# Layer-norm scale of a conditioned FFN: root and reciprocal replaced by a power and a diagonal sum on GpSimd

## The chip, the cores and the metric

The kernel runs on one core of one Trainium2 chip. The metric is the time of one execution on the device in microseconds (us).

## The reference

Input x has 4 sequences of 1024 rows with D = 1024 columns. All arithmetic is float32.

```python
xr = x.reshape(Bx, Tx, 8, LATENT)                                # LATENT = 128
h = jnp.einsum('btel,elf->btef', xr, W1) + b1                    # 8 experts, 128 -> 512
h = jax.nn.gelu(h, approximate=False)
y = (jnp.einsum('btef,efl->btel', h, W2) + b2).reshape(Bx, Tx, Dx)   # 512 -> 128
eo = jax.nn.silu(emb) @ emb_W + emb_b
scale, shift = jnp.split(eo[:, None, :], 2, axis=-1)
# _layernorm: (h - mu) * jax.lax.rsqrt(var + 1e-5) * g + b, over the 1024 columns
hn = _layernorm(y, ln_g, ln_b) * (1.0 + scale) + shift
return x + jax.nn.silu(hn) @ out_W + out_b
```

## The kernel before

Every matmul is made from three float32r products: each operand is split into a high and a low part (names ending in `_hi` and `_lo`), ScalarE or VectorE rounds the high part and VectorE subtracts it for the low part. The order of every engine's work is written out by hand in its own block, with counting semaphores between them.

**First stage (to about 354 us).** 32 items n, one for each of the 8 groups g and 4 sequences t; each has 4 steps c over the 512 hidden columns, so 128 steps m. For a step TensorE runs `first` (W1, L923) and `second` (W2, L939), ScalarE the gelu (L489), VectorE the split of its result (L663, L665). A finished item, a transposed block of y with 128 columns by 1024 rows, goes to `y_scratch` in DRAM. Between the steps VectorE computes dot products for the conditioning vector.

**Second stage (from about 354 us).** y is transposed here: columns lie on the partitions. A pair p is 256 rows of y (two row tiles q = 2p and 2p + 1), a tile of 128 partitions x 8 groups x 256. There are 16 pairs and 32 row tiles. For a pair:

- VectorE sums the 8 groups into `mean_total` (L738 to L748), GpSimd sums that over the partitions (L427, `mean_of`), so every partition has the sum for each of the 256 rows; VectorE subtracts the mean (`centre`, L753).
- ScalarE squares (L509), VectorE sums into `var_total` (L758 to L766), GpSimd sums over the partitions into `var_all` (L434, `var_of`).
- ScalarE takes the root of var / D + eps (`root`, L523), for which it changes its table before and after (L519, L601, and L559 for pair 0); VectorE takes the reciprocal (`invert`, L770) and multiplies both halves of y by it (`norm`, L775).
- ScalarE applies scale, shift and silu (L589) and rounds (L514), VectorE makes the low part (`rest_s`, L793).
- TensorE multiplies with out_W (`project`, L949), 48 matmuls for a row tile q; the last row tile is cut into pieces (`project_pieces`, L1001). VectorE adds the result to x (`finish`, L868), x having been given the bias by a DMA with addition from GpSimd's queue (`add_bias`, L440).

VectorE's loop over i is what sets the order. Pass i does: `finish(2i - 1)`, the inverse and norm of pair i + 1, the mean sums of pair i + 2, the low part of the first half of pair i + 1, `finish(2i)`, the centring of pair i + 2, the low part of the second half, the variance sums of pair i + 2. `finish` also holds the tail sums (L698): products for the conditioning vectors of the last two sequences, three ahead of an odd q and one ahead of an even q up to q = 12, then one or two up to q = 19. TensorE starts row tile q when `finish(q - 2)` is done and, for even q, when the low part of its pair is there. GpSimd's loop does in pass i `mean_of(i + 2)`, `add_bias(2i + 2)`, `var_of(i + 2)`, `add_bias(2i + 3)`. Pairs 0 and 1 are done beside the first stage, at items written out one by one (the norm of pair 0 at item 27, before the splits of later steps).

## Time and profile before

| what | value |
| --- | --- |
| median of 3 runs | 706.13 us (706.08 to 706.57) |
| span of the profiled execution, first to last instruction | 704.2 us |
| TensorE busy | 700.5 us, 99% of the span |
| VectorE busy | 603.7 us, 86% |
| ScalarE busy | 469.3 us, 67% |
| GpSimd busy | 104.1 us, 15% |
| moved by DMA | 133.22 MB, 189 GB/s on average |
| chain that ended last | TensorE 99% of the span |

The profile is of one execution. Its span leaves out what lies around the first and the last instruction; the median of the runs is the time with that. The names of lines are those of the program before. An engine's busy share says how full it is over the whole span; which wait counts is read from the timelines of one pass and from the chain. In a timeline, what stands in square brackets is the time for which the engine was idle before the row and what ended it.

### The profile page before, as it was taken

What the parts mean: (1) busy time and instruction counts of PE and PEld (TensorE: products, weight loads), DVE (VectorE), ACT (ScalarE), POOL (GpSimd) and SP (SyncE); (2) the same over time, 40 slices, a digit from 0 to 9 for tenths busy, and PEclk for the clock granted to TensorE, in tenths of its full rate; (3) what the DMA queues carried; (4) which work ended last, traced back from release to release, by engine and by line L of the source; (5) the groups of instructions that cost most, each with busy time, mean ns of one, the idle gap of its engine ahead of it and who ended that gap; (6) DMA issues with size and microseconds to landing.
All of it is one profiled execution on the core that took longest, in us unless ns stands there. A gap on an engine that the chain in (4) does not pass through costs nothing.

```text
span 704.2 us, 8302 instructions
## 1 busy us (share of the span) xinstructions
PE 700.5 (99%) x3082; PEld 577.9 (82%) x3082; DVE 603.7 (86%) x725; ACT 469.3 (67%) x526; POOL 104.1 (15%) x68
## 2 busy tenths in 40 slices
PE   9999999999999999999999999999999999999998
PEld 6888888888888888888888888888888888888887
DVE  6888999999999989899887999999999978677512
ACT  7898888888878879888883456454656454555500
POOL 0000000000000011100121332423232432322100
PEclk9999999999999999999999999999999999999999
DMA  6766557344232531332789687887699877565531
GB/s 240 247 232 207 187 203 231 109 169 150 90 121 90 209 120 61 120 107 104 210 293 301 183 279 233 275 256 246 219 293 264 256 217 210 183 176 143 156 120 60
DMA packets 51880, 133.22 MB, mean 189 GB/s; under 512 B 4096, under 2 KB 25216, under 8 KB 49408
## 3 DMA queue, kind: packets, MB, share of 16 engines
q1 hardware_dynamic: 46944, 115.79, 46.9%
q0 software_dynamic: 4608, 16.78, 12.3%
q8 instruction: 24, 0.39, 0.2%
q10 hardware_dynamic: 288, 0.13, 0.1%
q14 instruction: 16, 0.13, 0.1%
HBM read 82.35 MB, written 33.55 MB: 165 GB/s over the span
## 4 chain that ended last, share of the span: by engine, by line
PE 99%; DMA 0%; ACT 0%; DVE 0%; issue 0%; DVEq 0%
PE psum L949 48%; PE psum L939 25%; PE psum L923 25%; PE psum L1001 2%; DMA wraw<-in_W 0%; PE psum L971 0%; ACT W L534 0%; DVE res L901 0%; DVEq L125 0%
## 5 line engine op out<-in xcount | busy, mean ns | idle before, releaser
L665 DVE TENSOR_TENSOR g_lo<-g_raw,g_hi 128x1024 fp32r<-128x1024 f32 x128 | 158.4, 1239 | 27.9 <-ACT g_hi L495 25.3
L489 ACT ACTIVATE g_raw<-psum,cols 128x1024 f32<-128x1024 f32 x128 | 142.9, 1116 | 34.1 <-PE psum L923 24.9
L949 PE MATMUL psum<-oW_hi,s_lo 128*128 128x512 f32 x496 | 152.7, 389 | 0.0
L949 PE MATMUL psum<-oW_hi,s_hi 128*128 128x512 f32 x496 | 152.7, 389 | 0.0
L949 PE MATMUL psum<-oW_lo,s_hi 128*128 128x512 f32 x496 | 152.6, 389 | 0.0
L939 PE MATMUL psum<-g_hi,W 128*128 128x512 f32 x512 | 136.8, 389 | 0.0
L923 PE MATMUL psum<-xT_hi,W 128*128 128x512 f32 x508 | 135.8, 389 | 0.0
L939 PEld LDWEIGHTS psum<-g_hi,W 128*128 128x128 f32 x512 | 96.1, 188 | 20.0
L923 PEld LDWEIGHTS psum<-xT_hi,W 128*128 128x128 f32 x508 | 95.3, 188 | 19.8
L949 PEld LDWEIGHTS psum<-oW_hi,s_hi 128*128 128x128 f32 x496 | 93.1, 188 | 19.4
L949 PEld LDWEIGHTS psum<-oW_hi,s_lo 128*128 128x128 f32 x496 | 93.1, 188 | 19.3
L949 PEld LDWEIGHTS psum<-oW_lo,s_hi 128*128 128x128 f32 x496 | 93.1, 188 | 19.3
L589 ACT ACTIVATE yb<-yb,mod_c,mod_a 128x256 f32<-128x256 f32 x120 | 62.3, 590 | 56.6 <-DVE yb L775 56.6
L427 POOL PARTITION_ALL_REDUCE mean_all<-mean_total x16 | 41.2, 2576 | 384.0 <-DVE mean_total L748 384.0
L939 PE MATMUL psum<-g_lo,W 128*128 128x512 f32 x256 | 78.8, 389 | 0.0
L868 DVE TENSOR_TENSOR res<-psum,res 128x1024 f32<-128x1024 f32 x31 | 37.8, 1219 | 47.6 <-PE psum L949 47.6
L923 PE MATMUL psum<-xT_lo,W 128*128 128x512 f32 x254 | 78.2, 389 | 0.0
L495 ACT CAST g_hi<-g_raw 128x1024 fp32r<-128x1024 f32 x63 | 66.3, 1052 | 8.1 <-PE psum L939 6.7
L509 ACT ACTIVATE sq<-yb 128x1024 f32<-128x1024 f32 x32 | 34.0, 1062 | 36.6 <-DVE yb L753 35.6
L434 POOL PARTITION_ALL_REDUCE var_all<-var_total x16 | 35.8, 2237 | 144.0 <-DVE var_total L766 144.0
L698 DVE SCALAR_TENSOR_TENSOR tail_out<-tail_cols,tail_cond 128x1024 f32<-128x1024 f32 x32 | 52.4, 1666 | 4.6 <-DMA tail_cols<-in_emb_T 4.6
L939 PEld LDWEIGHTS psum<-g_lo,W 128*128 128x128 f32 x256 | 47.9, 188 | 10.1 <-DVE g_lo L665 0.2
(77 smaller groups left out, 679.8 us busy)
## 6 DMA issues: line engine op xcount, KB each, us to landing
y_scratch<-y_stage SPq DMA_DIRECT2D x32, 512.0 KB, 3.1
yb<-y_scratch SPq DMA_DIRECT2D x16, 1024.0 KB, 4.8
res<-in_x SPq DMA_DIRECT2D x32, 512.0 KB, 6.1
res<-out_b_all POOLq DMA_DIRECT2D x32, 512.0 KB, 4.5
xT_raw<-in_xT SPq DMA_DIRECT2D x31, 512.0 KB, 4.3
out<-res SPq DMA_DIRECT2D x31, 512.0 KB, 4.1
tail_cols<-in_emb_T SPq DMA_DIRECT2D x24, 512.0 KB, 7.2
wraw<-in_out_W SPq DMA_DIRECT2D x16, 256.0 KB, 4.9
```

Source lines behind the costliest of these rows:

```text
L427: nc.gpsimd.partition_all_reduce(mean_all[:], mean_total[:], P, bass.bass_isa.ReduceOp.add).then_inc(mean_done, 1)
L434: nc.gpsimd.partition_all_reduce(var_all[:], var_total[:], P, bass.bass_isa.ReduceOp.add).then_inc(var_done, 1)
L489: nc.scalar.activation(g_raw[:, m % 2], ring(m), ACT.Gelu, bias=cols[:, R_B1 + k:R_B1 + k + 1]).then_inc(gelu_done, 1)
L495: nc.scalar.copy(g_hi[:, m % 2], g_raw[:, m % 2]).then_inc(ghi_act, 1)
L509: nc.scalar.activation(sq[:, half_of(h)], yb[p % 3][:, half_of(h)], ACT.Square).then_inc(squared, 1)
L589: nc.scalar.activation(yb[p % 3][:, g], yb[p % 3][:, g], ACT.Silu, scale=mod_a[:, b, g:g + 1], bias=mod_c[:, b, g:g + 1]).then_inc(silu_do ...
L665: nc.vector.tensor_tensor(g_lo[:, m % 2], g_raw[:, m % 2], g_hi[:, m % 2].bitcast(F32), ALU.subtract).then_inc(glo_done, 1)
L698: nc.vector.scalar_tensor_tensor(tail_out[i % 2][:], tail_cols[l % SLOTS][:], 1.0, tail_cond[:, b - EARLY], ALU.mult, ALU.mult, accum_out= ...
L868: nc.vector.tensor_tensor(res[:, q % 4], proj(q), res[:, q % 4], ALU.add).then_inc(out_ready, 1)
L923: mm = nc.tensor.matmul(ring(m)[:, half], W[:, g % WS, w, cut], v[:, n % 2, half], start=(k == 0), stop=(k == 2))
L939: mm = nc.tensor.matmul(y_psum(n)[:, half], W[:, g % WS, w, cut], v[:, m % 2, half], start=(c == 0 and k == 0), stop=(c == C - 1 and k == 2))
L949: mm = nc.tensor.matmul(proj(q)[:, half], v[:, g, cut], w[:, g, half], start=(g == 0 and k == 0), stop=(g == G - 1 and k == 2))
```

## The change

`root` on ScalarE and `invert` on VectorE go. GpSimd, after its sum over the partitions, issues a DMA that takes the 256 values of one partition and lays them out as two per partition (`var_spread`, 128 x 2), scales them and adds eps, takes them to the power -0.5, writes them onto a diagonal (`rstd_diag`, 128 x 256, zero but for the two columns that belong to the partition), and sums that over the partitions, so that every partition again has all 256 values (`rstd`). `norm` reads `rstd` from SBUF for every pair. The outputs of the tail products, which nothing reads, go to PSUM banks 4 to 7 instead of SBUF. Some small buffers move.

```diff
-        eps = at("eps", [P, 1], S0 + 5600)
         mean_all = at("mean_all", [P, TP], S0 + 5632)
-        var_all = at("var_all", [P, TP], S0 + 6656)
-        std = at("std", [P, TP], S0 + 7680)
+        var_all = at("var_all", [P, TP], S0 + 1536)
+        rstd = at("rstd", [P, TP], S0 + 7680)
         mean_total = at("mean_total", [P, TP], S0 + 8704)
         var_total = at("var_total", [P, TP], S0 + 9728)
-        rstd0 = at("rstd0", [P, TP], S0 + 1536)
+        exponent = at("exponent", [P, 2], S0 + 5600)
+        var_spread = at("var_spread", [P, 2], S0 + 4096)
+        rstd_spread = at("rstd_spread", [P, 2], S0 + 4128)
+        rstd_diag = at("rstd_diag", [P, TP], S0 + 6656)
...
-        tail_out = [at(f"tail_out{k}", [P, K], o) for k, o in enumerate((S0, R0 + 32 * KB))]
...
+        exponent_set = sem("exponent_set")
...
+        var_landed = sem("var_landed")
+        var_scaled = sem("var_scaled")
+        rstd_power = sem("rstd_power")
+        rstd_placed = sem("rstd_placed")
...
+        tail_out = [pair(4), pair(6)]
...
-        rstd_ps = psum[:, 5, 0:TP]
...
             def var_of(p):
                 pool.wait_ge(var_tree, 3 * p + 3)
-                if p >= 1:
-                    pool.wait_ge(std_done, p)
                 nc.gpsimd.partition_all_reduce(var_all[:], var_total[:], P, bass.bass_isa.ReduceOp.add
                                                ).then_inc(var_done, 1)
+                pool.wait_ge(var_done, p + 1)
+                pool.dma_start(var_spread[:], var_all[0:1].rearrange("o (q j) -> o q j", j=2)).then_inc(var_landed, 16)
+
+            def rstd_of(p):
+                pool.wait_ge(var_landed, 16 * (p + 1))
+                nc.gpsimd.tensor_scalar(var_spread[:], var_spread[:], 1.0 / D, LN_EPS, ALU.mult, ALU.add
+                                        ).then_inc(var_scaled, 1)
+                if p == 0:
+                    pool.wait_ge(exponent_set, 1)
+                pool.wait_ge(var_scaled, p + 1)
+                nc.gpsimd.tensor_tensor(rstd_spread[:], var_spread[:], exponent[:], ALU.pow).then_inc(rstd_power, 1)
+                pool.wait_ge(rstd_power, p + 1)
+                if p >= 1:
+                    pool.wait_ge(rstd_done, p)
+                nc.gpsimd.affine_select(rstd_diag[:].rearrange("p (q j) -> p q j", j=2),
+                                        rstd_spread[:].unsqueeze(1).to_broadcast([P, P, 2]),
+                                        pattern=[[1, P], [0, 2]], channel_multiplier=-1, base=0,
+                                        compare_op=ALU.is_equal, fill=0.0).then_inc(rstd_placed, 1)
+                pool.wait_ge(rstd_placed, p + 1)
+                if p >= 1:
+                    pool.wait_ge(normed, 2 * p)
+                nc.gpsimd.partition_all_reduce(rstd[:], rstd_diag[:], P, bass.bass_isa.ReduceOp.add
+                                               ).then_inc(rstd_done, 1)
...
+            nc.gpsimd.memset(exponent[:], -0.5).then_inc(exponent_set, 1)
             mean_of(0)
             mean_of(1)
             var_of(0)
+            rstd_of(0)
             var_of(1)
+            rstd_of(1)
             pool.wait_ge(out_b_landed, 16)
             for q in range(2):
...
                 if i + 2 < NP:
                     var_of(i + 2)
+                    rstd_of(i + 2)
                 if 2 * i + 3 < QN:
                     add_bias(2 * i + 3)
...
-            def root(p):
-                if p == 0:
-                    act.wait_ge(eps_set, 1)
-                nc.scalar.preload_act_table(ACT.Sqrt)
-                act.wait_ge(var_done, p + 1)
-                if p >= 1:
-                    act.wait_ge(rstd_done, p)
-                nc.scalar.activation(std[:], var_all[:], ACT.Sqrt, bias=eps[:], scale=1.0 / D).then_inc(std_done, 1)
...
-                if (n, c) == (26, 0):
-                    root(0)
-                    nc.scalar.preload_act_table(ACT.Gelu)
...
-            root(1)
             nc.scalar.preload_act_table(ACT.Silu)
...
                     square(p + 1, 1)
-                    root(p + 1)
-                    nc.scalar.preload_act_table(ACT.Silu)
...
-                nc.vector.scalar_tensor_tensor(tail_out[i % 2][:], tail_cols[l % SLOTS][:], 1.0, tail_cond[:, b - EARLY],
+                nc.vector.scalar_tensor_tensor(tail_out[i % 2], tail_cols[l % SLOTS][:], 1.0, tail_cond[:, b - EARLY],
...
-            def invert(p, rstd):
-                dve.wait_ge(std_done, p + 1)
-                nc.vector.reciprocal(rstd, std[:]).then_inc(rstd_done, 1)
-
-            def norm(p, h, rstd):
+            def norm(p, h):
                 dve.wait_ge(rstd_done, p + 1)
                 part = yb[p % 3][:, half_of(h)]
-                nc.vector.tensor_tensor(part, part, rstd.unsqueeze(1).to_broadcast([P, HG, TP]), ALU.mult
+                nc.vector.tensor_tensor(part, part, rstd[:].unsqueeze(1).to_broadcast([P, HG, TP]), ALU.mult
                                         ).then_inc(normed, 1)
...
-                if (n, c) == (27, 1):
-                    invert(0, rstd0[:])
                 if (n, c) == (27, 2):
-                    norm(0, 0, rstd0[:])
+                    norm(0, 0)
...
                 if p < NP:
-                    invert(p, rstd_ps)
-                    norm(p, 0, rstd_ps)
-                    norm(p, 1, rstd_ps)
+                    norm(p, 0)
+                    norm(p, 1)
```

GpSimd's queue, the second half of pass 0, from the program before (rows named ISA with a tile are sums over the partitions; `res` is the row tile that gets the bias):

```order
L440 DMA res<-out_b_all 128x1024 [waits res_landed2]
L434 ISA var_all<-var_total 128x256 [waits std_done,var_tree]
L440 DMA res<-out_b_all 128x1024 [waits res_landed3]
L427 ISA mean_all<-mean_total 128x256 [waits centred,mean_tree]
```

The same place in the changed program, from the first bias DMA to the second:

```order
L466 DMA res<-out_b_all 128x1024 [waits res_landed2]
L437 ISA var_all<-var_total 128x256 [waits var_tree]
L440 DMA var_spread<-var_all 128x1x2 [waits var_done]
L444 ISA
L444 TENSOR_SCALAR var_spread<-var_spread 128x2 [waits var_landed]
L449 TENSOR_TENSOR rstd_spread<-var_spread,exponent 128x2 [waits var_scaled]
L453 AFFINE_SELECT rstd_diag<-rstd_spread 128x256 [waits rstd_done,rstd_power]
L460 ISA
L460 ISA rstd<-rstd_diag 128x256 [waits normed,rstd_placed]
L466 DMA res<-out_b_all 128x1024 [waits res_landed3]
```

Eight rows now stand between the two bias DMAs where one stood; two of them are ISA rows without a tile, one ahead of the scale and one ahead of the second sum.

VectorE's queue, from the last variance sum of pair 3 into pass 2, before:

```order
L766 TENSOR_TENSOR var_total<-sq 128x256 [waits var_done,var_tree]
L698 SCALAR_TENSOR_TENSOR tail_out_95,emb_dots<-tail_cols_100,tail_cond 128x1024 [waits tail_dot]
L698 SCALAR_TENSOR_TENSOR tail_out_96,emb_dots<-tail_cols_101,tail_cond 128x1024 [waits tail_landed3,tail_dot]
L698 SCALAR_TENSOR_TENSOR tail_out_95,emb_dots<-tail_cols_102,tail_cond 128x1024 [waits tail_landed4,tail_dot]
L868 TENSOR_TENSOR res<-psum,res 128x1024 [waits res_biased3,proj_done]
L770 RECIPROCAL psum<-std 128x256 [waits std_done]
L775 TENSOR_TENSOR yb_84<-yb_84,psum 128x1024 [waits rstd_done] x2
L738 TENSOR_TENSOR sq<-yb_91 128x1024 [waits y_landed1]
```

And in the changed program (`psum` as the output of L711 is the tail products' new place):

```order
L779 TENSOR_TENSOR var_total<-sq 128x256 [waits var_done,var_tree]
L711 SCALAR_TENSOR_TENSOR psum,emb_dots<-tail_cols_100,tail_cond 128x1024 [waits tail_dot]
L711 SCALAR_TENSOR_TENSOR psum,emb_dots<-tail_cols_101,tail_cond 128x1024 [waits tail_landed3,tail_dot]
L711 SCALAR_TENSOR_TENSOR psum,emb_dots<-tail_cols_102,tail_cond 128x1024 [waits tail_landed4,tail_dot]
L875 TENSOR_TENSOR res<-psum,res 128x1024 [waits res_biased3,proj_done]
L784 TENSOR_TENSOR yb_86<-yb_86,rstd 128x1024 [waits rstd_done] x2
L751 TENSOR_TENSOR sq<-yb_93 128x1024 [waits y_landed1]
```

The reciprocal is gone, the norm waits for GpSimd's second sum, and the rows behind it are the same.

## Rows read from the trace of the kernel before

**Rows 1.** The page, part 1: busy us of each engine (share of the span), instructions.
```profile
PE 700.5 (99%) x3082; PEld 577.9 (82%) x3082; DVE 603.7 (86%) x725; ACT 469.3 (67%) x526; POOL 104.1 (15%) x68
```

**Rows 2.** The windows: busy us of PE, PEld, DVE, ACT, POOL; granted clock; DMA share; GB/s.
```profile
400.00:450.00 50.00, 50.00 (x222) 41.42 (x221) 49.62 (x54) 24.97 (x34) 14.98 (x9) 1.00 0.80 251
```

**Rows 3.** The chain that ended last, its end: start us, us, what.
```profile
354.54 335.92 PE psum L949 x1482
690.46 10.96 PE psum L1001 x54
```

**Rows 4.** The timeline of VectorE, one pass: start us, us, engine, line, operation.
```profile
396.54 0.43 DVE L766 TENSOR_TENSOR var_total<-sq 128x256 f32<-128x256 f32 x1
...
402.35 1.74 DVE L770 RECIPROCAL psum<-std 128x256 f32<-128x256 f32 x1
404.13 2.35 DVE L775 TENSOR_TENSOR yb<-yb,psum 128x1024 f32<-128x1024 f32 x2
...
409.85 2.12 DVE L698 SCALAR_TENSOR_TENSOR tail_out<-tail_cols,tail_cond 128x1024 f32<-128x1024 f32 x1
...
418.49 0.42 DVE L766 TENSOR_TENSOR var_total<-sq 128x256 f32<-128x256 f32 x1
```

**Rows 5.** The timeline of ScalarE in the same stretch.
```profile
399.79 0.51 ACT L523 ACTIVATE std<-var_all,eps 128x256 f32<-128x256 f32 x1 [3.97 <-POOL var_all L434]
```

**Rows 6.** The timeline of GpSimd, the same stretch and near the end.
```profile
397.07 2.69 POOL L434 PARTITION_ALL_REDUCE var_all<-var_total  x1 [6.65 <-DVE var_total L766]
400.88 0.89 POOL L440 DMA_DIRECT2D res<-out_b_all  x1 [1.13 <-DMA res<-in_x]
...
610.59 1.79 POOL L434 PARTITION_ALL_REDUCE var_all<-var_total  x1 [6.84 <-DVE var_total L766]
...
622.04 2.69 POOL L427 PARTITION_ALL_REDUCE mean_all<-mean_total  x1 [6.69 <-DVE mean_total L748]
```

**Rows 7.** The timeline of VectorE, the first pairs.
```profile
288.33 0.43 DVE L766 TENSOR_TENSOR var_total<-sq 128x256 f32<-128x256 f32 x1
...
312.41 1.22 DVE L775 TENSOR_TENSOR yb<-yb,rstd 128x1024 f32<-128x1024 f32 x1
...
332.33 0.42 DVE L766 TENSOR_TENSOR var_total<-sq 128x256 f32<-128x256 f32 x1
...
355.70 2.35 DVE L775 TENSOR_TENSOR yb<-yb,psum 128x1024 f32<-128x1024 f32 x2
...
370.70 0.42 DVE L766 TENSOR_TENSOR var_total<-sq 128x256 f32<-128x256 f32 x1
```

**Rows 8.** The timeline of VectorE, the last pairs.
```profile
617.26 2.35 DVE L775 TENSOR_TENSOR yb<-yb,psum 128x1024 f32<-128x1024 f32 x2
...
625.21 1.22 DVE L868 TENSOR_TENSOR res<-psum,res 128x1024 f32<-128x1024 f32 x1 [2.15 <-PE psum L949]
...
631.82 0.43 DVE L766 TENSOR_TENSOR var_total<-sq 128x256 f32<-128x256 f32 x1
...
660.78 2.35 DVE L775 TENSOR_TENSOR yb<-yb,psum 128x1024 f32<-128x1024 f32 x2
665.29 1.23 DVE L793 TENSOR_TENSOR s_lo<-yb,s_hi 128x1024 fp32r<-128x1024 f32 x1 [2.16 <-ACT s_hi L514]
```

**Rows 9.** The instructions of L427 on GpSimd's queue.
```profile
L427 POOLq MODIFY_POOL_CONFIG  x2: 11/11/11, 0.8 to 0.8; - x2
```

**Rows 10.** DMA issues: KB each, median us to landing; and one issue on SyncE's queue.
```profile
res<-out_b_all POOLq DMA_DIRECT2D x32, 512.0 KB, 4.5
...
tail_cols<-in_emb_T SPq DMA_DIRECT2D x24, 512.0 KB, 7.2
wraw<-in_out_W SPq DMA_DIRECT2D x16, 256.0 KB, 4.9
emb_out<-in_emb_T SPq DMA_DIRECT2D x2, 2048.0 KB, 10.3
...
2.10 0.43 SPq L338 DMA_DIRECT2D cols<-in_vectors  x1
```

More of the change, by code:

```diff
@@ L194, in cond_ffn_program @@
         W1_HI, W1_LO, W2_HI, W2_LO = range(4)
-        eps_set = sem("eps_set")
+        exponent_set = sem("exponent_set")
         vec_landed = sem("vec_landed")
@@ L246, in cond_ffn_program @@
         var_done = sem("var_done")
-        std_done = sem("std_done")
+        var_landed = sem("var_landed")
+        var_scaled = sem("var_scaled")
+        rstd_power = sem("rstd_power")
+        rstd_placed = sem("rstd_placed")
         rstd_done = sem("rstd_done")
@@ L608, in _ @@
         def _(dve):
-            nc.vector.memset(eps[:], LN_EPS).then_inc(eps_set, 1)
             def split_raw(j, h):
@@ L846, in _ @@
                 if (n, c) == (28, 2):
-                    norm(0, 1, rstd0[:])
+                    norm(0, 1)
                 if (n, c) == (29, 0):
```

## The prediction

> **What bounds the kernel now.** I read the engines' busy time first. TensorE is busy for 700.5 of 704.2 us [rows 1], and from 354.54 us to the end the chain that ended last is matmuls alone: 1482 in 335.92 us, then the last 54 in 10.96 us [rows 3]. That is 226.7 ns each, so one row tile q (48 matmuls) takes 10.88 us and one pair of tiles 21.76 us. The last pair starts at 690.46 - 10.88 = 679.58 us, and 24.6 us later the span ends.
>
> So the reader's next question is what may come late for TensorE. In the windows VectorE is busy 49.62 of 50 us from 400 to 450 us, at a granted clock of 1.00 [rows 2]. The timeline of VectorE shows the loop there, one pair per pass: var_total of a pair ends at 396.97 us, the norm starts at 404.13, the next var_total ends at 418.91 [rows 4]. I call the first stretch C (var_total to norm, 7.16 us now) and the second W (norm to next var_total, 14.78 us). VectorE runs in order and the norm of pair p is ahead of all work for pair p+1, so a pass takes C + W (21.94 us here) once the norm has to wait, and TensorE cannot get a pair faster than that. C holds the sum on GpSimd and the root, for which ScalarE had sat idle 3.97 us [rows 5]; meanwhile VectorE did three tail sums and an add.
>
> **What the change removes.** ScalarE loses 16 roots of 0.51 us and their table loads, VectorE 16 reciprocals of 1.74 us [rows 4, 5]. Both are worth nothing in time: TensorE does not wait now, so its 700 us are the cover, and no faster than they can it go. The reciprocal's 1.74 us per pass only shorten C where the norm does not wait for something else. The tail products write to PSUM instead of SBUF. One in two took 2.12 us [rows 4], the others 1.22; I take 1.2 for all, so W falls by 0.9 to 13.9 us. If the move does nothing W stays 14.8 and the sum below rises by 8 us.
>
> **What it adds, step by step, in C.** All of it is one chain on GpSimd, behind which VectorE's norm is queued.
> - First sum over partitions: from 396.97 to 399.76 us (397.07 + 2.69) [rows 4, 6]: 2.8 us.
> - A wait for it and the issue of the 8-byte-per-partition DMA: 0.9 us as the other DMA issues of this queue [rows 6], and 0.1 between: 1.0.
> - The ISA row before the scale, with no tile. In the program before there is one such row, and the trace names what L427 did there: MODIFY_POOL_CONFIG, two records of 11 ns [rows 9]. So it changes the code that GpSimd runs, and the change has two per pair, 32 in all, between the sums (one set) and the elementwise work (the other). What it costs is not in the trace: the one before stands at 0.8 us, long ahead of the first sum. Below, 11 ns. Above, code has to come from memory: 10.3 us, the longest landing of any transfer [rows 10]. I take the transfer that is nearest in kind and place, a read from HBM in this same stretch: 7.2 us for tail_cols, and 0.4 for its issue [rows 10]: 7.6 us. The load stands ahead of the scale's wait, so the landing of the small DMA (at most the 4.5 us of the 512 KB ones on this queue) lies beside it.
> - Scale, power and diagonal. No row shows them. Below, nothing; above, three times the 1.79 us of a sum [rows 6], 5.4. The diagonal has 128 x 256 elements like the reciprocal, 1.74 us, the other two have two columns: I take 1.75 + 0.85 with the waits between = 2.6.
> - Second ISA row: nothing lies beside it, the sum behind it needs both: 7.6.
> - Second sum: 1.79 (VectorE stands still, and the sum took that where VectorE was idle) [rows 6], and 0.1 to the norm: 1.9.
>
> C = 2.8 + 1.0 + 7.6 + 2.6 + 7.6 + 1.9 = **23.5 us**. The three tail sums and the add, 5.4 us (396.97 to 402.35), lie beside it.
>
> By the Trainium skill ("GPSIMD Engine Reference", section "Instruction dispatch") the first call into freshly loaded code pays about 6 us (5.95) that no row of a profile shows. No run here has it yet; with 5.95 for each of the two the sum below would be 866.
>
> **The sum.** Pairs 0 and 1 lie under the first stage: var_total of pair 0 ends at 288.76, so its norm can start at 312.3, and starts now at 312.41; pair 1: 332.75 + 23.5 = 356.2, now 355.70 [rows 7]. Neither costs anything, with no margin. var_total of pair 2 then ends at 371.12 as before [rows 7]. From there 13 passes lead to pair 15: nine with one tail sum (W 13.9), four without. For those W was 631.82 + 0.42 - 617.26 = 14.98 [rows 8], of which 2.15 was a wait for TensorE that goes; the mean's sum ends at 624.73 [rows 6] and the add would end at 624.3, so 0.4 comes back: 13.3.
>
> - var_total of pair 15: 371.1 + 13 x 23.5 + 9 x 13.9 + 4 x 13.3 = 854.9 us; its norm starts at 878.4.
> - From the norm to the last pair on TensorE: 666.52 - 660.78 = 5.74 to the low part [rows 8], and the add of the tile before, 1.2: 7.0. TensorE starts at 885.4.
> - 24.6 us to the end: 910.0. The median of the runs shown, 706.13, is 1.9 above the span of 704.2: **912 us**.
>
> In short the time is 583 + 14 C (912 - 14 x 23.5 = 583), as long as that is above 706. Other queues: the bias DMAs stand behind the rstd chain, but their rows are used a pass later; the next mean's sum comes 4.7 us after the norm starts and only one issue of 0.9 is ahead of it. SyncE gets no new step.
>
> **Rivals.** *Cheap switches.* If an ISA row costs its 11 ns, C is 2.8 + 1.0 to 4.5 (now the DMA's landing shows) + 2.6 + 1.9 = 8.3 to 11.8, and the time 706 to 748, say 725. For it: the 11 ns. Against: a change of code with nothing moved.
>
> *Not slower.* One mechanism: the chain fits where VectorE has other work. It decides at C = 8.8, where 583 + 14 C is 706: below it TensorE never waits. It needs free switches, a DMA that shows no more than its issue, and small steps of 0.5 together: C = 6.2. Against it: 32 rows that cost nothing and three GpSimd steps at less than a sum's third.
>
> *Half clock.* TensorE now idles 23.5 + 13.9 - 21.8 = 15.6 us per pass, as nowhere in this trace, where the granted clock is 1.00 [rows 2]. At 1.2 GHz a matmul would take 453 ns and a pair 43.5 us, more than the pass of 37.4: TensorE would bound again, 14 pairs from 400 us, 1010 us. A slow start alone is hidden by the idle time, save in the last pair. The Trainium skill ("TensorE: Matmul & The Clock Gate", section "HAM oscillation — how this bites in real kernels") says that an array left idle between bursts falls back to 1.2 GHz; I expect to see that at the head of each pair.
>
> *Dearer switches.* At 10.3 + 0.4 each, C = 29.7: 14 x 6.2 = 87 more. The norm of pair 0 comes 6 us late in the first stage, ahead of splits that TensorE needs, 5 more: 1004. With 4.9 + 0.4, a 256 KB read [rows 10], C = 18.9: 848. The small steps at their ends move it by -36 and +39.
>
> **Chances.** Two real switches with a time of 840 to 1005: 0.80, the forecast, 912. Cheap switches 0.07 (725). Over 1005, by dearer switches or the half clock: 0.10. Not slower: 0.03. The range takes in the ends of the switch but not both unknowns at their ends together: 840 to 1005. About 0.2% is what a measurement of this kernel can tell from no change: faster by more 0.01, within 0.02, slower 0.97.
>
> **What would show it.** Right: VectorE idle about 18 us before each norm, ended by the GpSimd sum into rstd; gaps of some 7 to 8 us on GpSimd, one before the scale and one before the second sum, with nothing in them; TensorE idle some 15 us once per pair from 400 us on; a pass of 37 us; a span of 910. Wrong: gaps under 2 us (cheap switches), a gap only on the first pair (the code stays), or matmuls at 450 ns through whole pairs. If the tail products still take 2.1 us, W was mis-sized.

## The result and the profile after

| | before | changed |
| --- | --- | --- |
| median on the same chips | 706.33 us (706.08 to 706.57, 4 runs) | 895.0 us (893.18 to 897.51, 4 runs) |
| ratio | | 1.2673, 95% interval 1.2652 to 1.2695 |
| span of the profiled execution | 704.2 us | 895.8 us |

The kernel is slower by 189 us. The forecast was 912 us with a range of 840 to 1005.

The page of the changed kernel, part 1 (busy us of each engine) and part 4 (the chain that ended last), against [rows 1, 3]:

```profile
PE 737.0 (82%) x3082; PEld 600.8 (67%) x3082; DVE 578.9 (65%) x708; ACT 421.1 (47%) x479; POOL 180.7 (20%) x149
...
PE 42%; issue 20%; DVE 19%; POOL 11%; DMA 7%; ACT 1%; POOLq 0%; SPq 0%; DVEq 0%; ACTq 0%
```

TensorE was 99% of the chain before; now it is 42% of it, and a fifth is "issue", time in which nothing is recorded at all. The waits of the changed kernel (engine, line, what it waited for, us in total, times, longest) say where that sits:

```profile
DVE yb L784 <- POOL rstd L460: 244.1, 15, 20.3
...
PE psum L955 <- DVE res L875: 155.2, 14, 12.7
POOL var_spread L444 <- issue: 123.9, 16, 8.6
...
POOL rstd L460 <- issue: 97.2, 16, 7.2
```

VectorE waits for `rstd` ahead of the norm, TensorE waits for VectorE, and GpSimd has two gaps per pair, 7.7 and 6.1 us on average. Ahead of each stand only short records on GpSimd's queue, two `MODIFY_POOL_CONFIG` per gap (ns, shortest, median and longest; first and last start), the same that [rows 9] shows once:

```profile
L444 POOLq MODIFY_POOL_CONFIG  x32: 37/42/47, 292.5 to 844.0; - x32
L460 POOLq MODIFY_POOL_CONFIG  x32: 5/11/11, 302.8 to 854.1; - x32
```

Nothing is recorded in the gaps themselves. One pass on GpSimd's timeline (start us, us, engine, line, operation; idle time before in brackets) answers to [rows 6]:

```profile
448.50 2.69 POOL L437 PARTITION_ALL_REDUCE var_all<-var_total  x1 [6.64 <-DVE var_total L779]
451.48 0.60 POOL L440 DMA_DIRECT2D var_spread<-var_all  x1 [0.30 <-POOL var_all L437]
459.58 0.18 POOL L444 TENSOR_SCALAR var_spread<-var_spread 128x2 f32<-128x2 f32 x1 [7.50 <-issue]
459.85 0.74 POOL L449 TENSOR_TENSOR rstd_spread<-var_spread,exponent 128x2 f32<-128x2 f32 x1
460.66 1.25 POOL L453 TENSOR_SCALAR_AFFINE_SELECT rstd_diag<-rstd_spread 128x256 f32<-128x256 f32 x1
467.89 1.81 POOL L460 PARTITION_ALL_REDUCE rstd<-rstd_diag  x1 [5.98 <-issue]
```

The same pass on VectorE's timeline, against [rows 4]:

```profile
447.97 0.42 DVE L779 TENSOR_TENSOR var_total<-sq 128x256 f32<-128x256 f32 x1
448.31 1.23 DVE L711 SCALAR_TENSOR_TENSOR psum<-tail_cols,tail_cond 128x1024 f32<-128x1024 f32 x1
...
449.46 2.11 DVE L711 SCALAR_TENSOR_TENSOR psum<-tail_cols,tail_cond 128x1024 f32<-128x1024 f32 x1
...
452.67 1.21 DVE L875 TENSOR_TENSOR res<-psum,res 128x1024 f32<-128x1024 f32 x1
469.74 2.36 DVE L784 TENSOR_TENSOR yb<-yb,rstd 128x1024 f32<-128x1024 f32 x2 [15.85 <-POOL rstd L460]
...
475.47 2.12 DVE L711 SCALAR_TENSOR_TENSOR psum<-tail_cols,tail_cond 128x1024 f32<-128x1024 f32 x1
...
484.11 0.42 DVE L779 TENSOR_TENSOR var_total<-sq 128x256 f32<-128x256 f32 x1
```

The end of var_total at 448.39 and the norm at 469.74 give C = 21.35 us here; over the 14 passes of pairs 2 to 15 its mean is 21.32 (20.6 to 22.6). W, from the norm to the end of the next var_total, is 14.79 (484.53 - 469.74). A pass takes 36.1 us where it took 21.94.

The windows of two pairs of that stretch (busy us of PE, PEld, DVE, ACT, POOL; granted clock; DMA share; GB/s), against [rows 2]:

```profile
411.80:448.90 37.10, 26.23 (x105) 21.09 (x105) 21.61 (x25) 8.27 (x12) 12.07 (x10) 0.85 0.48 154
448.90:486.00 37.10, 25.03 (x99) 20.13 (x98) 21.11 (x25) 8.26 (x12) 12.63 (x10) 0.82 0.52 167
```

TensorE is idle for 11 to 12 us of each 37, and its granted clock is no longer 1.00. Its timeline at the head of one pair, and at the head of the last pair, shows why (two matmuls per row):

```profile
407.04 1.22 PE L955 MATMUL psum<-oW_hi,s_hi 128*128 128x512 f32 x2 [9.50 <-DVE res L875]
408.06 1.05 PE L955 MATMUL psum<-oW_lo,s_hi 128*128 128x512 f32 x2
...
413.02 0.62 PE L955 MATMUL psum<-oW_lo,s_hi 128*128 128x512 f32 x2
...
868.62 1.22 PE L955 MATMUL psum<-oW_hi,s_hi 128*128 128x512 f32 x2 [9.61 <-DVE res L875]
```

The window of 408 to 410 us has a granted clock of 0.50, the lower level of 1.2 GHz, and a row of two matmuls starts 0.85 us after the one before, about 426 ns each; from 413 us on it is 0.46 us, 227 ns each. Every pair begins so, after 9.5 to 12.7 us of idle time, and after 8 to 14 matmuls the clock is at 2.4 GHz again.

The second unexpected place is pair 2. The first two rows are of VectorE's and ScalarE's timelines, the third is the landing of `tail_cond`'s two DMAs (shortest, median, longest):

```profile
374.14 1.23 DVE L771 TENSOR_TENSOR sq<-sq 128x1024 f32<-128x1024 f32 x1 [4.58 <-ACT sq L539]
```
```profile
370.21 2.01 ACT L613 ACTIVATE tail_cond<-tail_cond 128x1024 f32<-128x1024 f32 x2 [6.12 <-DMA tail_cond<-in_cond]
```
```profile
DMA to landing us min/median/max: 11.4/12.1/12.7
```

ScalarE waited 6.12 us for that DMA ahead of the squares of pair 2, so var_total of pair 2 ended at 376.55 us, not at 371.12 as before [rows 7]. In the kernel before the same DMAs landed after 6.0 to 6.7 us. What moved beside them is the bias DMA of the first two row tiles: in the kernel before it was issued at 341.11 us, and here it had to wait on GpSimd's queue until the second sum of pair 1 was done, and went out just ahead of `tail_cond`. The first row is from before, the other two are of the changed kernel:

```profile
341.11 1.94 POOL L440 DMA_DIRECT2D res<-out_b_all  x2 [6.46 <-DMA res<-in_x]
...
356.39 1.97 POOL L466 DMA_DIRECT2D res<-out_b_all  x2
...
356.97 1.56 SPq L395 DMA_DIRECT2D tail_cond<-in_cond  x2
```

### The profile page after: what moved, and what is told of

The parts are those of the page before. It is cut to its first block, busy times and chain, and to the rows that moved or that the text cites. A ratio compares the mean times of both kernels' runs of the same rounds, so it can differ in the third digit from the quotient of the medians.

```text
span 895.8 us, 8385 instructions
## 1 busy us (share of the span) xinstructions
PE 737.0 (82%) x3082; PEld 600.8 (67%) x3082; DVE 578.9 (65%) x708; ACT 421.1 (47%) x479; POOL 180.7 (20%) x149
## 4 chain that ended last, share of the span: by engine, by line
PE 42%; issue 20%; DVE 19%; POOL 11%; DMA 7%; ACT 1%; POOLq 0%; SPq 0%; DVEq 0%; ACTq 0%
PE psum L945 19%; PE psum L929 19%; DMA var_spread<-var_all 5%; POOL var_all L437 4%; DVE yb L784 4%; DVE yb L766 3%; POOL rstd L460 3%; DVE psum L711 2%; DVE s_lo L802 2%; POOL rstd_diag L453 2%; DVE sq L771 2%; DVE sq L751 2%; PE psum L955 2%; DMA tail_cond<-in_cond 1%; PE psum L1007 1%
## 5 line engine op out<-in xcount | busy, mean ns | idle before, releaser
L955 PE MATMUL psum<-oW_hi,s_hi 128*128 128x512 f32 x496 | 168.1, 422 | 155.2 <-DVE res L875 155.2
L955 PEld LDWEIGHTS psum<-oW_hi,s_hi 128*128 128x128 f32 x496 | 100.5, 206 | 181.9 <-DVE res L875 161.2
L784 DVE TENSOR_TENSOR yb<-yb,rstd 128x1024 f32<-128x1024 f32 x32 | 37.9, 1221 | 244.1 <-POOL rstd L460 244.1
L678 DVE TENSOR_TENSOR g_lo<-g_raw,g_hi 128x1024 fp32r<-128x1024 f32 x128 | 160.5, 1255 | 27.9 <-ACT g_hi L525 25.1
L955 PE MATMUL psum<-oW_lo,s_hi 128*128 128x512 f32 x496 | 164.0, 414 | 0.0
L955 PE MATMUL psum<-oW_hi,s_lo 128*128 128x512 f32 x496 | 162.0, 409 | 0.0
L955 PEld LDWEIGHTS psum<-oW_lo,s_hi 128*128 128x128 f32 x496 | 100.8, 203 | 22.7
L955 PEld LDWEIGHTS psum<-oW_hi,s_lo 128*128 128x128 f32 x496 | 100.1, 202 | 22.3
L711 DVE SCALAR_TENSOR_TENSOR psum<-tail_cols,tail_cond 128x1024 f32<-128x1024 f32 x32 | 52.7, 1681 | 4.3 <-DMA tail_cols<-in_emb_T 4.3
L929 PEld LDWEIGHTS psum<-xT_lo,W 128*128 128x128 f32 x254 | 47.7, 188 | 9.9
```

Of the source, the lines that this page charges most:

```text
L678: nc.vector.tensor_tensor(g_lo[:, m % 2], g_raw[:, m % 2], g_hi[:, m % 2].bitcast(F32), ALU.subtract).then_inc(glo_done, 1)
L711: nc.vector.scalar_tensor_tensor(tail_out[i % 2], tail_cols[l % SLOTS][:], 1.0, tail_cond[:, b - EARLY], ALU.mult, ALU.mult, accum_out=emb ...
L784: nc.vector.tensor_tensor(part, part, rstd[:].unsqueeze(1).to_broadcast([P, HG, TP]), ALU.mult).then_inc(normed, 1)
L929: mm = nc.tensor.matmul(ring(m)[:, half], W[:, g % WS, w, cut], v[:, n % 2, half], start=(k == 0), stop=(k == 2))
L955: mm = nc.tensor.matmul(proj(q)[:, half], v[:, g, cut], w[:, g, half], start=(g == 0 and k == 0), stop=(g == G - 1 and k == 2))
```

## The experiments

Two theories to begin with. **Code changes**: the two gaps are GpSimd changing between the code of the sums and the code of the elementwise operations; they go if no elementwise operation but the diagonal stands between the sums. **Rival, the chain itself**: the gaps are the landing of the small DMA, or the waits between short operations, and stay if only the operations are taken away. A second question is what the removals, the PSUM outputs and the order around the chain are worth. C, W and the gaps below are read from the timelines of VectorE and GpSimd. C and the gaps are means over the passes of pairs 2 to 15, in which the changed kernel has gaps of 7.75 and 6.09 us; the kernel before ran beside them at medians of 706.3 to 706.6 us. In the short diffs "..." marks what is left out.

**1. No code change.** Scale and power go, the diagonal takes the spread variance.

```diff
-                nc.gpsimd.tensor_scalar(var_spread[:], var_spread[:], 1.0 / D, LN_EPS, ALU.mult, ALU.add
...
-                nc.gpsimd.tensor_tensor(rstd_spread[:], var_spread[:], exponent[:], ALU.pow).then_inc(rstd_power, 1)
...
-                                        rstd_spread[:].unsqueeze(1).to_broadcast([P, P, 2]),
+                                        var_spread[:].unsqueeze(1).to_broadcast([P, P, 2]),
```

> Left out: the scaling with eps and the power, so the norm multiplies by the plain sum of squares; the DMA, the diagonal and both sums stay. GpSimd then needs one set of code only and its queue has no code change in the loop. My theory (the two code changes are most of C): C = 2.8 first sum + 0.9 DMA issue + 3.0 landing (now nothing covers it) + 1.3 diagonal + 1.9 second sum = 9.9 us instead of 21.3; the chain still ends just above TensorE's pace (9.9 + 14.8 = 24.7 against 21.76), so 371.5 + 14 x 9.9 + 9 x 14.8 + 4 x 13.4 + 6.9 + 25 = 729, about 730 us. Rival (the arithmetic on GpSimd, the power above all, is what costs; the empty stretches belong to it): C falls by scale and power alone, 1.0 us, and the time to 881 us. Rival (the landing of the small DMA fills the first gap and would be as long here): C about 17, 830 us.

Measured: 724.99 us, ratio 1.0258 (1.0242 to 1.0274), C 9.24. GpSimd's timeline of one pass:

```profile
446.59 2.69 POOL L437 PARTITION_ALL_REDUCE var_all<-var_total  x1 [6.64 <-DVE var_total L772]
449.58 0.58 POOL L440 DMA_DIRECT2D var_spread<-var_all  x1 [0.30 <-POOL var_all L437]
451.84 1.24 POOL L446 TENSOR_SCALAR_AFFINE_SELECT rstd_diag<-var_spread 128x256 f32<-128x256 f32 x1 [1.67 <-DMA var_spread<-var_all]
453.17 1.79 POOL L453 PARTITION_ALL_REDUCE rstd<-rstd_diag  x1
```

Both gaps are gone, though DMA, diagonal and second sum are all still there: the diagonal needs no change of code beside the sums, and the DMA from its issue to the diagonal is worth 2.3 us in this pass (its landing took 1.9 to 6.2 us, 2.9 in the median), hidden beside the first code change in the changed kernel. 170 of the 189 us hang on the scale and the power, with all that they bring.

**2. The code changes without the work.** Scale and power go, but one addition of constants, whose result nothing reads, stands in their place.

```diff
-                pool.wait_ge(var_landed, 16 * (p + 1))
-                nc.gpsimd.tensor_scalar(var_spread[:], var_spread[:], 1.0 / D, LN_EPS, ALU.mult, ALU.add
...
+                nc.gpsimd.tensor_tensor(rstd_spread[:], exponent[:], exponent[:], ALU.add)
+                pool.wait_ge(var_landed, 16 * (p + 1))
```

> As the run with one set of code (scaling and power left out), but GpSimd adds two columns of constants into a buffer that nobody reads ahead of the diagonal, and that addition needs the other set of code: both code changes are back, with no power. My theory: C = 2.8 + 0.9 + 7.5 + 0.3 + 1.3 + 6.1 + 1.9 = 20.8 us, the time about 886 us. Rival (the arithmetic costs): the same as with one set of code, within 0.3 us per pair, so 5 us more than that run.

Measured: 883.72 us, 1.2512 (1.2486 to 1.2539), C 20.44, gaps 7.83 and 6.07. An addition of 0.18 us brings back 159 us. So it is the alternation of code that costs, and not the power (0.74 us). It is not the wait for the DMA either: here the addition that ends the first gap stands ahead of that wait.

**3. The small DMA from ScalarE's queue**, issued behind the squares; GpSimd issues only the bias DMAs.

```diff
-                pool.wait_ge(var_done, p + 1)
-                pool.dma_start(var_spread[:], var_all[0:1].rearrange("o (q j) -> o q j", j=2)).then_inc(var_landed, 16)
...
+            def spread(p):
+                act.wait_ge(var_done, p + 1)
+                act.dma_start(var_spread[:], var_all[0:1].rearrange("o (q j) -> o q j", j=2)).then_inc(var_landed, 16)
...
                     square(p + 1, 1)
+                    spread(p + 1)
```

> The changed kernel with the small DMA issued from ScalarE's queue instead of GpSimd's. The first code change took 7.7 us per pair, the second 6.1. Theory A (a code change has to wait until GpSimd's own DMA has been carried out): the first falls to 6.1 and the issue of 0.6 and 0.3 goes, C -2.5 us, 14 x 2.5 = 35 us less, 860 us. Theory B (the first set is simply longer to load, and the DMA doesn't matter to it): only the issue goes, C -0.9, 12 us less, 882 us. In both, the DMA of ScalarE's queue lands in the shadow of the code change.

Measured: 882.83 us, 1.2497 (1.2476 to 1.2518), C 20.26, gaps 7.77 and 5.91. The 0.9 us of wait and issue go from each pass, the gap stays. The first change is not longer than the second because a DMA was issued ahead of it.

**4. The add of the row tile ahead of its tail sums.** It tests whether the tail products of 2.1 us are long because of their output or because of GpSimd's sum beside them.

```diff
             def finish(q):
+                dve.wait_ge(proj_done, q + 1)
+                dve.wait_ge(res_biased[q % 4], 16 * (q // 4 + 1))
+                nc.vector.tensor_tensor(res[:, q % 4], proj(q), res[:, q % 4], ALU.add).then_inc(out_ready, 1)
                 for i in range(tail_done(q - 1), tail_done(q)):
                     tail_sum(i)
...
-                nc.vector.tensor_tensor(res[:, q % 4], proj(q), res[:, q % 4], ALU.add).then_inc(out_ready, 1)
```

> The changed kernel with finish() turned round: the add of the row tile first, the tail products after it. In both traces every tail product of 2.1 us instead of 1.2 runs beside a GpSimd sum over partitions, and the sum takes 2.7 instead of 1.8 us when a VectorE operation with two inputs in SBUF runs as it starts. Theory (the two keep each other out of SBUF): after var_total comes the add, which has one input in PSUM, so the first sum takes 1.8 us and C falls by 0.9 in some 10 to 12 passes; the even tail product starts 1.2 us later, W falls by up to 0.9 in 9 passes. Time 895 - 10 - 8 = about 877 us. Rival (one in two tail products is slow by its own addresses): the same count of slow ones, and 893 to 897 us.

Measured: 897.32 us, 1.2697 (1.2652 to 1.2742). The part on VectorE came as expected: all 32 tail products take 1.2 us (mean 1239 ns), GpSimd's variance sum 1.79 us in every pass (mean 1788 ns), and W is 13.9 in the nine passes. But C rose to 21.88, which gave the 8 us back. One pass on GpSimd's timeline, SyncE's queue, and the window of the gap (busy times, clock, DMA share, GB/s):

```profile
453.44 0.60 POOL L440 DMA_DIRECT2D var_spread<-var_all  x1 [0.30 <-POOL var_all L437]
463.33 0.18 POOL L444 TENSOR_SCALAR var_spread<-var_spread 128x2 f32<-128x2 f32 x1 [9.29 <-issue]
```
```profile
452.41 0.34 SPq L404 DMA_DIRECT2D out<-res  x1
```
```profile
453.44:463.33 9.89, 9.89 (x46) 8.18 (x45) 2.51 (x6) 0.00 (x0) 0.60 (x2) 1.00 0.85 299
```

The earlier add frees SyncE's store and the loads behind it at 452.41 us, right ahead of the first change: it takes 9.06 us on average (up to 10.9) where it took 7.75, while the second, with no traffic, takes 5.85. The time landed beside the rival's 893 to 897 us, but by another cause than the rival's. That the burst stretches the change is argued and not shown: in this order the tail products also run beside more of the change (in the pass above 1.8 us of it, 0.7 in the changed kernel), and no run held the burst back with this order and the changes in place.

**5. The squares of pair 2 ahead of the conditioning silus** on ScalarE.

```diff
+                if p + 1 < NP:
+                    square(p + 1, 0)
+                    square(p + 1, 1)
                 if i == 0:
                     act.wait_ge(tail_cond_landed, 2 * 16)
...
-                if p + 1 < NP:
-                    square(p + 1, 0)
-                    square(p + 1, 1)
```

> The changed kernel with the squares of pair 2 ahead of the two silus of the conditioning vectors on ScalarE. var_total of pair 2 ended at 376.55 us against 371.12 before; the squares stood behind silus that waited 6.1 us for a DMA. Theory: var_total of pair 2 ends at about 371.5, the time falls by 5 us to 890 us. Rival (the late norm of pair 1 carries over by itself): var_total of pair 2 stays within 1 us of 376.

Measured: 896.63 us, 1.2685 (1.266 to 1.271). var_total of pair 2 ended at 371.53 us, so the cause of the late pair 2 is the wait of ScalarE. It bought nothing: that pass now had C = 25.3, with both changes (8.9 and 8.6 us) under the start's traffic. In the profiled execution the norm of pair 15 came 3.9 us sooner (857.78 against 861.71), but that execution was the fastest of its four (893.43 us) and the one of the changed kernel the slowest of its four (897.51); the medians show no gain.

**6. The removals alone.** The kernel before without root, table loads and reciprocal; the norm reads the sum of the variance.

```diff
-                    root(p + 1)
-                    nc.scalar.preload_act_table(ACT.Silu)
...
-                    invert(p, rstd_ps)
```

> The kernel before without its roots, its 32 table loads and its 16 reciprocals: the norm multiplies by the plain sum of squares. It prices what the change takes away. Theory (worth nothing, TensorE sets the pace): 705.5 to 706.8 us, C down from 7.16 to about 5.4 us in the middle passes, with VectorE idle for the rest of the pass. Rival (VectorE at 99% from 400 to 550 us does hold the kernel up): up to 14 x 0.2 = 3 us less, 703 us.

Measured: 706.55 us, 1.0002 (0.9992 to 1.0011), C 5.39. All that the change could save is worth nothing here.

**7. Root on two columns, without code change.** The spread variance goes through ScalarE's root and VectorE's reciprocal, both on 128 x 2, then to the diagonal and the second sum.

```diff
+                nc.scalar.activation(rstd_spread[:], var_spread[:], ACT.Sqrt, bias=exponent[:, 0:1], scale=1.0 / D
...
+                nc.vector.reciprocal(rstd_inv[:], rstd_spread[:]).then_inc(rstd_power, 1)
...
-                nc.gpsimd.tensor_tensor(rstd_spread[:], var_spread[:], exponent[:], ALU.pow).then_inc(rstd_power, 1)
```

> A complete kernel with one set of GpSimd code: sum, small DMA, diagonal and second sum as in the change, but the root of the two columns on ScalarE (with its table loads again) and their reciprocal on VectorE. C = 9.24 us as measured with the arithmetic left out, + root 0.3 + reciprocal 0.2 + two handoffs 0.3 = 10.0; time 725 + 14 x 0.8 = 736 us. Rival (ScalarE's table load falls into C because the squares end only just before): C = 11.3, 754 us.

Measured: 735.37 us, 1.0415 (1.0396 to 1.0434), C 9.83, the small DMA landing after 3.3 us in the median (1.9 to 5.4). It computes all of the reference, as the changed kernel does, in 160 us less.

**8. A quiet first change.** SyncE holds the odd tile's store, and the loads behind it, until the second sum is done.

```diff
+                    if q % 2 == 1 and (q + 1) // 2 + 2 <= NP:
+                        sp.wait_ge(rstd_done, (q + 1) // 2 + 2)
```

> The changed kernel, in which SyncE's queue holds back the store of the odd row tile, and with it the next row load and two tail loads, until the sum into rstd of that pass is done. In the changed kernel 268 GB/s run during the first code change, 7.7 us, and nothing during the second, 6.1 us. Theory A (the code comes from memory and shares the DMA engines or HBM with the loads): the first falls to about 6.1, C from 21.3 to 19.7, and the time by up to 14 x 1.6 = 22 us, to 873 us, if the held loads don't come late for the tail products. Theory B (the first set of code is larger): the first stays at 7.7 and the time at 895 us.

Measured: 889.89 us, 1.2595 (1.2568 to 1.2623), C 20.84. With 0 to 87 GB/s beside it in 13 of the 14 passes (131 in the other) the first change still took 7.38 us, the second 5.98. So the first is 1.4 us longer by itself, and the traffic that was held back here was worth 0.4 us in the changed kernel. Experiment 4 lies 1.7 us above the quiet value.

**9. The repairs together.** Experiment 7 with the edits of 3 and 4; ScalarE's table for the root is loaded ahead of the issue of the small DMA.

```diff
-                pool.dma_start(var_spread[:], var_all[0:1].rearrange("o (q j) -> o q j", j=2)).then_inc(var_landed, 16)
...
+                act.dma_start(var_spread[:], var_all[0:1].rearrange("o (q j) -> o q j", j=2)).then_inc(var_landed, 16)
...
+                nc.vector.tensor_tensor(res[:, q % 4], proj(q), res[:, q % 4], ALU.add).then_inc(out_ready, 1)
                 for i in range(tail_done(q - 1), tail_done(q)):
                     tail_sum(i)
```

> The kernel with one set of GpSimd code and the root of two columns on ScalarE, and in addition the small DMA from ScalarE's queue and the add of the row tile ahead of the tail products. It asks whether the chain, once short enough, leaves no trace in the time. C = 9.83 - 0.9 (issue) - 0.5 (first sum 1.8 instead of 2.7 us in 8 of 14 passes) = 8.4 us, W 13.9 and 13.4 us: by the chain alone 372 + 14 x 8.4 + 178.6 + 6.9 + 24.6 + 1.9 = 702 us, which lies under TensorE's 706.3. Theory (C decides only above about 8.8 us): 706 to 710 us, TensorE busy 99%. Rival (the longer path with a DMA in it costs in any case, by the spread of its landing): 715 us or more.

Measured: 761.58 us, 1.0793 (1.0778 to 1.0807), worse than 7. W was 13.9 as expected, but C rose to 12.18, since the small DMA landed after 6.6 us (median; 1.9 to 8.7). One pass on ScalarE's timeline, then on SyncE's queue:

```profile
433.12 0.49 ACTq L540 DMA_DIRECT2D var_spread<-var_all  x1
440.32 0.29 ACT L548 ACTIVATE rstd_spread<-var_spread,exponent 128x2 f32<-128x2 f32 x1 [10.27 <-DMA var_spread<-var_all]
```
```profile
432.35 0.34 SPq L405 DMA_DIRECT2D out<-res  x1
432.74 0.43 SPq L337 DMA_DIRECT2D res<-in_x  x1
433.22 1.38 SPq L331 DMA_DIRECT2D tail_cols<-in_emb_T  x2
```

The 1 KB transfer is issued in the middle of four transfers of 512 KB. Two things had changed, the queue and the moment of the burst; the last three runs take them apart.

**10. Experiment 9 with the add late again** (7 and the edit of 3).

```diff
-                pool.dma_start(var_spread[:], var_all[0:1].rearrange("o (q j) -> o q j", j=2)).then_inc(var_landed, 16)
...
+                act.dma_start(var_spread[:], var_all[0:1].rearrange("o (q j) -> o q j", j=2)).then_inc(var_landed, 16)
```

> The kernel with the root on two columns, with one thing moved: the small DMA is issued from ScalarE's queue, the tail sums stay ahead of the add as in the kernel before. Nothing is left out of the computation. Theory (in the run with the repairs together the small DMA landed late because the earlier add let SyncE issue its store and loads at the same moment, and the small DMA stood behind their packets): with the add late again the DMA lands in about 3 us, C is about 9, and the time about 725 us. Rival (ScalarE's queue itself is served more slowly beside SyncE's transfers): landing 6 to 7 us, C about 12, about 765 us.

Measured: 737.21 us, 1.0433 (1.0417 to 1.0448), C 9.77, landing 2.7 us in the median. The queue is not the cause. The time came out 12 us over the theory's, 11 of them since the mean C is 9.77 and not 9. In five passes, those of pairs 2, 8, 11, 13 and 14, the small DMA landed after 4.5 to 6.5 us and C was 10.2 to 12.2; in the others C was 8.7 to 9.3. That these do not go lower is another floor, here on VectorE's and ScalarE's timelines:

```profile
409.86 1.21 DVE L898 TENSOR_TENSOR res<-psum,res 128x1024 f32<-128x1024 f32 x1
411.00 0.15 DVE L800 RECIPROCAL rstd_inv<-rstd_spread 128x2 f32<-128x2 f32 x1
414.39 2.36 DVE L805 TENSOR_TENSOR yb<-yb,rstd 128x1024 f32<-128x1024 f32 x2 [3.25 <-POOL rstd L452]
```
```profile
410.34 0.29 ACT L548 ACTIVATE rstd_spread<-var_spread,exponent 128x2 f32<-128x2 f32 x1 [5.90 <-DMA var_spread<-var_all]
```

The root is there before the reciprocal can run: VectorE is still at its tail sums and add (5.4 us) and needs 3.4 more to the norm, so C can't go below 8.8 in such a pass.

**11. Experiment 7 with the add first alone**, the small DMA on GpSimd's queue.

```diff
+                nc.vector.tensor_tensor(res[:, q % 4], proj(q), res[:, q % 4], ALU.add).then_inc(out_ready, 1)
                 for i in range(tail_done(q - 1), tail_done(q)):
                     tail_sum(i)
```

> The kernel with the root on two columns, with the other thing moved alone: the add of the row tile stands ahead of the tail sums, the small DMA stays on GpSimd's queue. Nothing is left out of the computation. Theory (the earlier add brings SyncE's burst onto the small DMA): landing about 6 us, C about 12, W 13.9 in the nine passes, about 760 us. Rival (it was ScalarE's queue): landing about 3, C about 10, W 13.9, about 720 us.

Measured: 752.42 us, 1.0651 (1.0635 to 1.0668), W 13.9, C 11.81, landing 6.2 us in the median. So the earlier burst of SyncE makes the small DMA late, whatever queue issues it: experiments 7, 9, 10 and 11 are the four combinations of queue and order.

**12. Experiment 9 with SyncE's burst held back** until the small DMA of that pass has landed.

```diff
+                    if q % 2 == 1 and (q + 1) // 2 + 2 <= NP:
+                        sp.wait_ge(var_landed, 16 * ((q + 1) // 2 + 2))
```

> The kernel with the repairs together (root on two columns, small DMA from ScalarE's queue, add ahead of the tail sums), and SyncE holds the odd row tile's store, and so the loads behind it, until the small DMA of that pass has landed. Nothing is left out of the computation. Theory (the burst is what delays the small DMA): landing about 2 us, C about 8.0, which is below 8.8, the point from which TensorE is not made to wait: 706 to 710 us. Rival (the held loads now come late for the tail sums or the adds that read them): W grows, over 715 us.

Measured: 718.41 us, 1.017 (1.0146 to 1.0195), W 13.9, C 9.02 (7.6 to 11.2), landing 3.2 us in the median. W did not grow, so the rival falls, but the landing is not always 2 us: in passes where SyncE's loads of the next tiles had gone out just before, it still was up to 5.4. TensorE sat idle for 8.3 us in all, between 443 and 583 us, and its busy time was 704.1 us, 3.6 more than in the kernel before: together about the 12 us by which the kernel is slower than the one before. It is the best of the versions with a diagonal, 43 us better than experiment 9, and still slower than the kernel before. No version here beats that one, in which TensorE is busy for 99% of the span.

## Why the prediction was right, and where it was off

The mechanism was the one forecast: VectorE's norm waits for a chain on GpSimd, two changes of GpSimd's code make up most of it, and TensorE waits for VectorE. The result, 895.0, lies 17 us below 912. Step by step, the terms of the sum against the profiled execution (897.5 us, the slowest of the four, so the last row is below zero):

| term | predicted | measured | in the sum |
| --- | --- | --- | --- |
| end of var_total of pair 2 | 371.1 us | 376.55 us | +5.4 |
| C, 14 times | 23.5 us | 21.32 us | -30.5 |
| W, nine passes | 13.9 us | 14.79 us | +8.0 |
| W, four passes | 13.3 us | 13.40 us | +0.4 |
| norm to last pair on TensorE | 7.0 us | 6.9 us | -0.1 |
| last pair to end | 24.6 us | 27.2 us | +2.6 |
| around the span, execution to median | +1.9 us | -0.8 us | -2.7 |

- **C.** In the pass shown, term by term: first sum 2.8 (2.8), wait and issue 0.9 (1.0), first change 7.5 (7.6), scale to diagonal 2.3 (2.6), second change 6.0 (7.6), second sum and handoff 1.85 (1.9). The step "second ISA row: 7.6" is the one mis-sized, by 1.5 us in each of 14 passes, 21 us of the 30. Another 5 us are the first sum: I took 2.8 us for all passes, and it took 1.79 instead of 2.69 in six of the 14, as the kernel before shows it at 610.59 us [rows 6]; the small steps at 2.3 and not 2.6 are 4 more. I had priced both changes alike, by a read from HBM in this stretch. The first was right to 0.1 us by luck, as far as the runs show: in the second change of the pass above the trace shows no DMA traffic at all, and experiment 8 shows the first at 7.4 us almost without traffic. By the Trainium skill ("GPSIMD Engine Reference", section "Instruction dispatch") the first call into freshly loaded code pays 5.95 us with nothing visible; the second change (6.0 us) agrees with it, the first (7.4 to 7.8) is longer, and the page does not distinguish them. An estimate by the page's figure alone was 866 us, the row gave 912, and 895 lies in between.
- **W.** The step "I take 1.2 for all, so W falls by 0.9" failed. The output went to PSUM, but both inputs are still read from SBUF, and every second product still took 2.1 us. Experiment 4 shows what it hangs on: with the add, which has one input in PSUM, beside the variance sum, neither that sum nor any product is long. In the pass above the sum starts at 448.50 while the first product runs (to 449.54), and takes 2.69 instead of 1.79; the second product then takes 2.11 and not 1.2. That is each waiting for the other in turn. The Trainium skill states that ("SBUF — State Buffer", section "SBUF: two separate sides"): a VectorE operation with two SBUF inputs and a GpSimd operation that reads SBUF lock each other out for a whole instruction, whichever starts first. The rows agree that each holds the other up, by 0.9 us on either side. They do not show a whole instruction for the product: it ends at 451.57, 0.4 us after the sum (451.19), and takes 1.2 us alone. I had named the other case, W 14.8 and 8 us more, as the one "if the move does nothing".
- **Pair 2.** "var_total of pair 2 then ends at 371.12 as before" took for granted that what moved nothing on VectorE's order moved nothing on ScalarE's waits. ScalarE's squares stand behind silus on a DMA, and this DMA landed after 12.7 us. What I had missed is that "the bias DMAs stand behind the rstd chain" matters at the start as well: held back by it, those of the first two row tiles went out 0.6 us ahead of this DMA. In the five runs in which they did so (the changed kernel and experiments 2, 4, 5 and 8) the DMA landed after 11.4 to 13.6 us; in the three in which they had gone out 14 us or more before (the kernel before, experiments 1 and 6) after 5.8 to 6.9. No run moved them alone. Experiment 5 shows that the wait is the cause of the 5.4 us, and also that mending it returns little, as the same traffic then stretches the next C.
- **The end.** "A slow start alone is hidden by the idle time, save in the last pair" held, and the last pair paid for it: 12 matmuls at up to twice their time are 2.4 of the 2.6 us. I had named it and not put it in the sum. TensorE's idle time per pair was 9.5 to 12.7 us and not some 15, as the pass is shorter and the slow head fills 2 to 3 us of it. The Trainium skill ("TensorE: Matmul & The Clock Gate", section "HAM oscillation — how this bites in real kernels") says that an array left idle between bursts falls back to 1.2 GHz; the granted clock of 0.50 at the head of the pairs agrees. The half clock rival, in which whole pairs run so, did not happen.
- **Removed work at nothing.** Right: experiment 6, 1.0002 (0.9992 to 1.0011).
- **Cheap switches.** Forecast at 725 us if the changes were free; experiment 1, which has none, is at 724.99. The two agree partly by luck, since W and pair 2 were worse and scale and power are left out there.
- **Not slower from C = 8.8 down.** That point stands on W = 13.9. With W at 14.8 the same sum gives 706 only for C near 8.2. In experiment 12, with W 13.9 and a mean C of 9.02, the sum gives 709 and the time is 718. A mean of C is not what decides: TensorE waited in the passes with C up to 10.6, and in the later ones, with C of 7.6 to 9.0, it did not wait and could not win the time back.

What stays open: why the first change is 1.4 us longer than the second when both are quiet, by which path code comes in, since the records show no transfer for it, and whether the burst is what stretched it in experiment 4. That traffic can stretch a change is seen best on the second change of pair 2, the one that has some beside it: 7.2 us with 172 GB/s in the changed kernel and 8.6 with 217 in experiment 5, but 5.8 with 3 in experiment 8, where the burst was held back. It isn't by its mean rate alone: in the changed kernel one first change with 345 GB/s beside it took 7.7 us, in experiment 4 six with 200 to 300 took 9.3 to 10.9.

## What to carry to other kernels

Before an operation moves to an engine whose operations come as loadable code, look at what its neighbours on that engine use: one addition of 0.18 us between two sums cost GpSimd 13 to 14 us per pass and made the chain 11.2 us longer, the same diagonal and sum without it cost nothing of the kind. Price a new chain against what now waits for it, and find first whether the removed work was on the path at all; here it was worth nothing. When a small transfer stands on the path, an improvement elsewhere that brings a burst of large ones forward can cost more than it gains, so its landing has to be read again after every reordering.

## What the runs showed of the hardware

- A change of GpSimd's code between the partition sums and plain elementwise operations took 7.4 to 7.8 us on average in one direction and 5.9 to 6.1 in the other, 8.6 in the second direction with 217 GB/s beside it, up to 10.9 in the first in experiment 4, and is recorded only as two `MODIFY_POOL_CONFIG` of 5 to 47 ns. The diagonal (affine select, 128 x 256, 1.25 us) needs no change beside the sums.
- On GpSimd a scale of 128 x 2 took 0.18 us and a power of 128 x 2 0.74 us. The root of 128 x 2 on ScalarE took 0.30 us against 0.51 for 128 x 256 [rows 5], the reciprocal on VectorE 0.17 against 1.74 [rows 4]: on the two columns the original pair of operations is the cheap one.
- A DMA of 8 bytes for each of 128 partitions landed after 1.9 us at best, 3 us in the median, and 6 to 9 us when issued among four of 512 KB.
- After 9.5 to 12.7 us of idle time TensorE started each pair at a granted clock of 0.50, with matmuls of 426 ns, which cost nothing while VectorE was the slower of the two.
